# State-space stage rewritten: packed keys and queries, taps on three engines, skip as a matmul, unrolled sequence loop

## The reference, cut to what matters

```
xBC = sum((xp[:, k:k + L, :] * conv_w[:, k] for k in range(D_CONV))) + conv_b   # 4 taps
xBC = silu(xBC);  X = x * dt[..., None]
Y = (Y_diag + Y_off).reshape(b, L, NHEADS, HEADDIM) + x * D[:, None]            # skip
y = y * silu(z)
y = y * rsqrt(mean(y * y, axis=-1, keepdims=True) + EPS) * norm_w
return einsum('bld,ed->ble', y, out_proj_w)
```

## Time and profile before

| what | value |
|---|---|
| time, median of 3 runs | 1439.13 us (1433.71 to 1442.06) |
| the profiled execution's own time | 1442.29 us |
| its span, first to last instruction | 1440.5 us |
| mean granted clock of TensorE | 0.885 |
| busy PE, DVE, ACT, POOL | 83%, 59%, 50%, 23% |
| stage `L1_attn`, from the trace | 284.6 to 381.9 us |

### The profile page before, as it was taken

One profiled execution on the slowest core, in us unless ns is written; L12 is line 12 of the kernel. 1 busy time (PEld: TensorE's weight loads), 2 busy tenths in 40 slices (PEclk: granted clock), 3 DMA queues, 4 the chain that ended last, 5 costly groups with the idle time before them and its releaser, 6 DMA issues. The chain is left out here.

```text
span 1440.5 us, 24196 instructions
## 1 busy us (share of the span) xinstructions
PE 1195.0 (83%) x8927; PEld 763.0 (53%) x8928; DVE 853.4 (59%) x2086; ACT 723.1 (50%) x1459; POOL 326.6 (23%) x337
## 2 busy tenths in 40 slices
PE   6997995459698996777887973989889988897998
PEld 4664553237465664336734743856434444465776
DVE  3564564767676547787786888358452555573111
ACT  2563552341275224586677772456566542564332
POOL 1333100013211003654556440130000034300000
PEclk9999897567899998687997995799899988899999
DMA  7000000010000000000000000061094800000000
GB/s 287 1 2 2 1 2 0 24 66 1 0 2 2 1 0 1 0 1 2 2 1 1 2 1 2 1 261 67 1 198 107 170 1 1 1 2 1 1 1 15
DMA packets 15203, 44.33 MB, mean 31 GB/s; under 512 B 1872, under 2 KB 4976, under 8 KB 14448
## 3 DMA queue, kind: packets, MB, share of 16 engines
q1 hardware_dynamic: 15088, 42.80, 10.0%
HBM read 42.01 MB, written 0.79 MB: 30 GB/s over the span
## 5 line engine op out<-in xcount | busy, mean ns | idle before, releaser
L863 DVE TENSOR_REDUCE L_xattn_top<-banks 128x4 f32<-128x512 f32 x128 | 80.7, 672 | 32.6 <-PE banks L709 32.6
L815 ACT ACTIVATE L_xattn_p<-L_xattn_p 128x512 f32<-128x512 f32 x128 | 76.0, 630 | 23.8 <-DVE L_xattn_p L868 23.7
L868 DVE TENSOR_TENSOR L_xattn_p<-banks,L_xattn_top 128x512 f32<-128x512 f32 x128 | 82.4, 686 | 4.8
L823 ACT ACTIVATE L_xattn_pT<-banks 128x512 f32<-128x512 f32 x128 | 70.0, 595 | 18.3 <-PE banks L722 18.0
L722 PE MATMUL banks<-w_const,L_xattn_p 128*128 128x128 f32 x512 | 70.4, 279 | 8.1 <-ACT L_xattn_p L815 8.1
L1398 DVE TENSOR_TENSOR L_ffn_a<-L_ffn_a,L_ffn_share 128x512 f32<-128x512 f32 x64 | 39.8, 685 | 60.5 <-DMA L_ffn_share<-L_ffn_shares 37.8
L709 PE MATMUL banks<-L_xattn_ks,L_xattn_qT 32*128 32x512 f32 x256 | 71.8, 647 | 1.8 <-ACT L_xattn_ks L799 1.1
L1631 ACT ACTIVATE L_ffn_aT<-banks,L_ffn_shift 128x512 f32<-128x512 f32 x64 | 43.3, 687 | 58.9 <-PE banks L1583 57.3
L1312 PE MATMUL banks<-L_ffn_a,region_a 128*128 128x512 f32 x136 | 68.4, 608 | 4.6 <-DVE L_ffn_a L1398 4.6
L1644 DVE SCALAR_TENSOR_TENSOR x<-banks,L_ffn_combine,x 128x128 f32<-128x128 f32 x64 | 18.1, 344 | 88.6 <-PE banks L1594 88.6
L1303 PE MATMUL banks<-hT,region_a 128*128 128x512 f32 x136 | 70.1, 622 | 0.0
(11 more groups left out here) (509 smaller groups left out, 2961.0 us busy)
## 6 DMA issues: line engine op xcount, KB each, us to landing
L_ffn_share<-L_ffn_shares SPq DMA_DIRECT2D x32, 512.0 KB, 9.7
region_b<-in_L_ffn SPq DMA_DIRECT2D x1, 6216.0 KB, 29.5
region_a<-in_L_ffn SPq DMA_DIRECT2D x1, 4416.0 KB, 13.4
region_b<-in_L_attn SPq DMA_DIRECT2D x1, 3150.5 KB, 10.3
region_a<-in_L_ffn SPq DMA_DIRECT2D x1, 3080.5 KB, 21.4
region_b<-in_L_attn SPq DMA_DIRECT2D x1, 1633.5 KB, 10.0
region_b<-in_L_xattn SPq DMA_DIRECT2D x1, 835.0 KB, 10.8
w_tables<-in_tables SPq DMA_DIRECT2D x1, 832.0 KB, 13.7
```

The lines of the kernel that those rows point to most:

```text
L815: nc.scalar.activation(p[:, m % 4, :], p[:, m % 4, :], ACT.Exp, scale=scale).then_inc(exped, 1)
L823: nc.scalar.activation(pT[:, n % 2, 2 * (P % 2) + e, :], tps[e][:], ACT.Copy).then_inc(pT_kept, 1)
L863: nc.vector.tensor_reduce(top[:, i, :], rows_of(score[i][:], 4), X, ALU.max)
L868: nc.vector.tensor_tensor(rows_of(p[:, i, :], 4), rows_of(score[i][:], 4), bc(top[:, i, :], 2, T), ALU.subtract).then_inc(centered, 1)
```

## The change

Only `state_space` is changed. The key and query tiles of sequences 0 to 3 go to partitions 0 to 63 and those of 4 to 7 to 64 to 127 (`bc2`), so each is 512 columns wide; small matmuls copy the constants to both halves. ACT scales by the last tap while it leaves PSUM; DVE adds the other three taps from PSUM for both of these tiles and for one tile of `x`; for the other, ACT writes all four scaled copies and POOL adds them. The skip is a product with a diagonal matrix, accumulated in PSUM with the sum. The square with its row sum is on ACT; the mean and the power are on POOL; the norm weight is folded into `w_out`; the row scale is applied in the last addition. The sequences run unrolled in one block, with more buffers and another order, and the first half of the next stage's norm is made at the end. The removed lines are those printed above; of the added ones the core:

```diff
@@ -2246,21 +2246,51 @@
...
+    xc = st.sb("xc", [128, 2, B, T])
+    bc2 = st.sb("bc2", [128, 2, 4, T])
+    scratch = st.sb("scratch", [128, 3, B, T])
...
+    const_bank, dt_bank, bc_bank = bank[6], bank[7], bank[0:2]
+    x_banks = (banks[:, 2:4, :].rearrange("p a (b t) -> p (a b) t", t=T), banks[:, 4:6, :].rearrange("p a (b t) -> p (a b) t", t=T))
+    z_bank = (bank[6], bank[7], bank[0], bank[1])
+    mixed, seg, sums, yps, out = bank[2:4], bank[4:6], bank[0:2], bank[6], bank[7]
+    G_AT, X_AT, LAST = 0, T, T + DI
+    INIT_AT, Y_AT = 0, DI
...
+            def add_taps():
+                for i in range(3):
+                    s = TAPS - 1 - i
+                    if i == 0:
+                        pool.wait_ge(pool_tapped, 4)
+                    else:
+                        pool.drain()
+                    last = nc.gpsimd.tensor_tensor(xc[:, 1, :, s:T], xc[:, 1, :, s:T], scratch[:, i, :, 0:T - s], ALU.add)
+                last.then_inc(pooled, 1)
+
+            def stage_decays(n):
+                if n >= 2:
+                    pool.wait_ge(exponents, n - 1)
+                nc.gpsimd.tensor_tensor(later[:, n % 2, :, :], bc(g.tables["gt"], 1, NH), bc(a[:, n, :], 2, T),
+                                        ALU.mult).then_inc(later_ready, 1)
...
+            add_taps()
+            pool.wait_ge(rates_ready, 1)
+            pool.wait_ge(g.tables.loaded, 16)
+            for s in range(B + 4):
+                if s < B:
+                    stage_decays(s)
+                if s == 10:
+                    ahead.invert(pool, 0)
+                if 0 <= s - 4:
+                    invert_norm(s - 4)
...
+            def copy_consts():
+                for half in range(2):
+                    rows, at = slice(DS * half, DS * half + DS), 0
+                    for source in (w["conv_w"][0:DS, 2 * TAPS:4 * TAPS], w["conv_b"][0:DS, 2:4], w["init"]):
+                        cols = source.shape[1]
+                        nc.tensor.matmul(const_bank[rows, at:at + cols], g.ident[0:DS, 0:DS], source, start=True, stop=True)
+                        at += cols
+                for j in range(2):
+                    last = nc.tensor.transpose(dt_bank[:, 128 * j:128 * j + 128], w["norm_w"][:, 128 * j:128 * j + 128], g.ident)
+                last.then_inc(consts_made, 1)
...
+            def project_bc(half):
+                norm.await_kept(pe, half)
+                for k in range(2):
+                    at = 2 * 128 + k * DS
+                    last = nc.tensor.matmul(bc_bank[k][DS * half:DS * half + DS, :], w["w_conv"][:, at:at + DS],
+                                            g.hT[:, half * HALF:(half + 1) * HALF], start=True, stop=True)
+                last.then_inc(proj, 1)
...
+            def start_sequence(n):
+                u, rows = n % 2, half_rows(n)
+                if n == 0:
+                    pe.wait_ge(silu_ready, 4)
+                    pe.wait_ge(g.tables.loaded, 16)
+                pe.wait_ge(later_ready, n + 1)
+                if n >= 2:
+                    pe.wait_ge(pairs, n - 1)
+                    pe.wait_ge(decay_ready, n - 1)
+                nc.tensor.matmul(mixed[u][:, G_AT:G_AT + T], bc2[rows, 0, n % 4, :], bc2[rows, 1, n % 4, :], start=True, stop=True)
+                nc.tensor.matmul(mixed[u][:, LAST:LAST + NH], g.tables["le"], a[:, n, :], start=True, stop=True)
+                for h in range(NH):
+                    nc.tensor.matmul(seg[u][:, h * T:(h + 1) * T], later[:, u, h, :], g.tables["le"], start=True, stop=True)
+                for j in range(2):
+                    last = nc.tensor.transpose(mixed[u][:, X_AT + 128 * j:X_AT + 128 * j + 128], xc[:, j, n, :], g.ident)
+                last.then_inc(exponents, 1)
+
+            def sum_sequence(n):
+                u, rows = n % 2, half_rows(n)
+                if n == 0:
+                    pe.wait_ge(z_kept, 4)
+                    pe.wait_ge(skips_ready, 1)
+                if n >= 2:
+                    pe.wait_ge(y_ready, n - 1)
+                nc.tensor.matmul(sums[u][:, INIT_AT:INIT_AT + DI], bc2[rows, 1, n % 4, :], twice[rows, 2 * TAPS + 2:TWICE],
+                                 start=True, stop=True)
+                for j in range(2):
+                    nc.tensor.matmul(sums[u][:, Y_AT + 128 * j:Y_AT + 128 * j + 128], xc[:, j, n, :], skips[:, j, :],
+                                     start=True, stop=False, skip_group_check=True)
+                    if j == 0:
+                        pe.wait_ge(pairs, n + 1)
+                    for h in (2 * j, 2 * j + 1):
+                        last = nc.tensor.matmul(sums[u][:, Y_AT + h * DH:Y_AT + (h + 1) * DH], decay[:, n % 3, h, :],
+                                                xdt[:, n % 3, h * DH:(h + 1) * DH], start=False, stop=True, skip_group_check=True)
+                last.then_inc(summed, 1)
...
+            def project_out(n):
+                pe.wait_ge(yT_kept, n + 1)
+                if n == 0:
+                    pe.wait_ge(out_ready, 1)
+                else:
+                    pe.wait_ge(added, n)
+                for j in range(2):
+                    last = nc.tensor.matmul(out[:, 0:D], yT[:, n % 2, j, :], w_out[:, j, :], start=(j == 0), stop=(j == 1))
+                last.then_inc(made, 1)
...
+            copy_consts()
+            norm.turn(pe, 0, bank[4])
+            project_bc(0)
+            norm.turn(pe, 1, bank[5])
+            make_rates()
+            project_bc(1)
+            project_x(1)
+            project_x(0)
+            for m in range(4):
+                make_z(m)
+            for s in range(B + 6):
+                if 0 <= s - 5 < B:
+                    project_out(s - 5)
+                if 0 <= s - 4 < B:
+                    turn_outputs(s - 4)
+                if 0 <= s - 2 < B:
+                    sum_sequence(s - 2)
+                if s < B:
+                    start_sequence(s)
+                if s == 11:
+                    pe.wait_ge(decay_ready, B)
+                    ahead.turn(pe, 0, seg[0])
...
+            def scale_x(j):
+                act.wait_ge(proj, 4 - j)
+                if j == 1:
+                    for i in range(3):
+                        nc.scalar.activation(scratch[:, i, :, :], x_banks[1], ACT.Copy, scale=taps_of(1, i)).then_inc(pool_tapped, 1)
+                nc.scalar.activation(xc[:, j, :, :], x_banks[j], ACT.Copy,
+                                     scale=taps_of(j, 3)).then_inc(pool_tapped if j == 1 else tapped, 1)
...
+            def exp_decays(n):
+                act.wait_ge(exponents, n + 1)
+                if n >= 3:
+                    act.wait_ge(summed, n - 2)
+                if n >= 4:
+                    act.wait_ge(y_ready, n - 3)
+                nc.scalar.activation(decay[:, n % 3, :, :], rows_of(seg[n % 2][:], NH), ACT.Exp)
+                nc.scalar.activation(decay0[:, n % 4, :], mixed[n % 2][:, LAST:LAST + NH], ACT.Exp).then_inc(decay_ready, 1)
...
+            def square(n):
+                act.wait_ge(y_ready, n + 1)
+                if n >= 2:
+                    act.wait_ge(rms_ready, n - 1)
+                nc.scalar.activation(sq[:, n % 2, :], y[:, n % 2, :], ACT.Square, accum_out=meansq[:, n:n + 1]).then_inc(squared, 1)
...
+            keep_consts()
+            norm.keep(act, 0, bank[4])
+            norm.keep(act, 1, bank[5])
+            scale_bc(0)
+            scale_bc(1)
             act.wait_ge(abs_ready, 1)
             nc.scalar.activation(e[:], e[:], ACT.Exp, scale=-1.0).then_inc(e_ready, 1)
+            scale_x(1)
             act.wait_ge(u_ready, 1)
             nc.scalar.activation(log_u[:], u1[:], ACT.Ln).then_inc(log_ready, 1)
+            scale_x(0)
+            silu_bc(0)
+            silu_bc(1)
             for m in range(4):
+                keep_z(m)
+            silu_x(0)
+            silu_x(1)
+            for s in range(B + 5):
+                if s < B:
+                    exp_decays(s)
+                if 0 <= s - 4 < B:
+                    keep_yT(s - 4)
+                if 0 <= s - 3 < B:
+                    square(s - 3)
+                if s == 11:
+                    ahead.keep(act, 0, seg[0])
...
+            def add_taps(tile):
+                for i in range(3):
+                    s = TAPS - 1 - i
+                    if i > 0:
+                        dve.drain()
+                    else:
+                        dve.wait_ge(tapped, 3 if tile == 0 else tile - 1)
+                    to = xc[:, 0, :, s:T] if tile == 0 else bc2[:, tile - 2, :, s:T]
+                    source = x_banks[0] if tile == 0 else rows_of(bc_bank[tile - 2][:], 4)
+                    last = nc.vector.scalar_tensor_tensor(to, source[:, :, 0:T - s], taps_of(tile, i), to, ALU.mult, ALU.add)
+                last.then_inc(convolved, 1)
...
+            def make_pairs(n):
+                u = n % 2
+                dve.wait_ge(decay_ready, n + 1)
```

(52 more changed lines are left out.)

301 lines of the change are left out of this document (100 added, 201 removed).

## The result

The changed kernel is slower: 1457.91 us in the median of 4 runs (1454.23 to 1462.39) against 1440.06 for the kernel before in the same comparison (1433.71 to 1442.06). The ratio is 1.0133, 95% interval 1.0084 to 1.0182. The forecast was 1421.2 us with a range of 1411 to 1434, so sign and size are both wrong. The profiled execution took 1461.45 us with a span of 1459.6 and a mean granted clock of 0.870 (before: 1442.29, 1440.5, 0.885). In all that follows the ratios and their intervals leave out executions more than 1.5% above the fastest of the same kernel (three of ten where the additions come later), while medians and ranges hold all of them.

The account below looks back on a forecast made before the run. DVE was taken to end the preparation and pace the sequences at the full clock, PE at the low clock. Gains 5.2 + 11.9 + 0.8 = 17.9 us from the 1439.1 us median gave 1421.2 us, range 1411 to 1434.

Parts of the forecast that it names:

- T1: End of `project_bc(1)` in the preparation, behind which all taps hang; forecast 300.3, or 299 to 302.7 depending on the clock.
- Preparation, 5.2 us forecast: Stage work before the first sequence: ACT's chain ends last, PE starts at 316.5 instead of 321.7; bounds 2.8 and 6.5.
- the 2.1 us for the rates: Preparation step on DVE: the rates follow ACT's Ln and take 2.1 us, ending at T1+9.8.
- rival 3: POOL's sums in the preparation slowed by DVE to 4 us each, first sequence 3.5 us later, 1424.7 us; chance 0.1.
- The stop, 1.35 us: PE's wait before the output projection in steps 5 to 8, for ACT's exponentials and `keep_yT`; 1.35 us each.
- The loop, 48.4 us forecast: Sequences from the first start to the last addition: 48.4 us against 60.25, gain 11.9, full step 5.65 us.
- with the low clock for 10 us as before: Assumption for the sequence loop: its first 10 us run at the low clock, as in the old loop.
- the 76%: PE's busy share in a new full loop step, 4.3 of 5.65 us, from which the full clock was taken as kept.
- Rival 2: PE bounds the sequence loop at the low clock throughout: loop 76.8 us, 10.6 us slower in all, 1450; chance 0.06.
- Its point of decision: Change loses if the loop behind its first 10 us is at the low clock over some two thirds of the time.
- The next stage, 0.8 us: From the last addition to the next stage's first reduction: 8.83 us against 9.67, gain 0.8, bounds 0 and 1.5.

Follow-up runs that it names:

- additions come later: Changed kernel with POOL's three additions waiting until the rates are ready; median 1435.92 us, ratio 0.9972 to the kernel before.
- the repetition: The changed kernel run again without any edit, for more runs; 1455.85 us, ratio 1.0099 to the kernel before.
- two and with four copies: Changed kernel with two or four in-place ACT copies between the last two Silus, starting the loop later; medians 1438.05 and 1453.34 us.
- busy entry: Changed kernel with five unused 512-column products filling PE's wait ahead of the first sequence; 1425.39 us, ratio 0.9903 to the kernel before.
- short products: Changed kernel with sixteen unused 128-column products ahead of the first sequence, in place of five of 512; 1424.92 us, ratio 0.9894.
- products too early: Changed kernel with five unused 512-column products placed 10 us earlier, ahead of the gate projections; 1455.5 us, ratio 1.0099.
- one copy: Changed kernel with one in-place ACT copy between the last two Silus, starting the loop later; median 1448.86 us, range 1436.15 to 1461.37.
- three copies: Changed kernel with three in-place ACT copies between the last two Silus; median 1458.64 us, none of six runs below 1455.

## Why the prediction was wrong, point by point

- **End of the first projections, T1.** Forecast 300.3; ACT's first scaled copy starts at 300.08. The number is right by luck. The constants were done at 286.7 instead of 289.3, the second half of the norm at 294.7 instead of 296.0 and the step sizes at 296.8 instead of 298.6; then the last projections took 3.3 us instead of 1.7, because the clock fell again (0.56 from 296.7 to 300.1).
- **Preparation, 5.2 us forecast, 1.7 measured.** The step that failed is the 2.1 us for the rates; they took 5.9 (307.96 to 313.86). I had looked at what DVE does to POOL, and rival 3 had it the wrong way round: POOL's additions weren't slowed (2.18 us each against 2.00 taken), but two of DVE's small products took 1.80 and 2.03 us beside them. Moving the additions removed this. The rule of the Trainium skill ("SBUF — State Buffer", "Who interferes with whom") that I quoted names an exclusion for the whole length and agrees with the trace; I priced only one of its two sides. Even the 1.7 us hung on the clock: in the repetition the step sizes take 3.55 us at 0.50 instead of 1.92 at the full clock, and the preparation takes 37.4 us from the stage's first DVE instruction to the first sequence, against 35.7 in the first profile and 37.1 before. There nothing is gained.
- **The stop, 1.35 us.** Measured 1.43 before PE's weight load at the low clock, 1.26 and 1.03 (load and product) at the full one, in the place named. Right. Taking it away gains 20 us in the median though its five stops add up to 6.6 us at most, so the rest comes through the clock.
- **The loop, 48.4 us forecast, 78.1 measured.** Here the prediction failed. Two sentences of it did: "with the low clock for 10 us as before" and, after the 76% that is "nearer to the second", "So I take it as kept to the drain". I took the busy share of PE as what decides the clock and copied the old entry to a new start. But the clock never came, with PE busy 28.00 of 28.00 us. My own rows warned of it: in the earlier trace rows PE is busy 13.40 of 13.40 us at 0.50, so a full busy share had not brought the clock up there for 13.4 us. With the entry at the full clock the loop takes 46.4 us and a step 6.0 against 5.65. My 48.4 held 10 us at the low clock; without them it would be about 43.4 (an estimate, at half speed), so the durations were some 7% too short as well: PE's own work in a step is 4.72 us, not 4.3. That is 3 us; the level is worth the 31.7 us between 46.4 and 78.1.
- **Rival 2 is what happened.** It gave a step of 9.95 us and a loop of 76.8; measured are 10.16 and 78.1. It gave 1450 us in all; the preparation's missing 3.5 us, 1.3 in the loop and the scatter behind the stage make up most of the rest. I gave it 0.06 because the old loop had been low for 21.4 of 50 us only. I had not asked whether the rise near 331.8 in the earlier trace rows would come to another stream with another start.
- **Its point of decision** was the share of the low clock, some two thirds of the time behind the first 10 us. This did not hold. The loops that come up at 340 to 343 take 56.7 and 56.5 us and are low for 12 to 13 of the 46 to 47 us behind the first 10, about a quarter; by my 28 us for all of it such a kernel would be some 10 us faster (an estimate), and they are level with the one before (ratios 0.9972 and 0.9978). What was missing is the preparation's gain and the longer steps. Those entered at the full clock are 1% faster.
- **The next stage, 0.8 us.** Measured 0.75 (8.92 against 9.67). Right, with PEclk at 0.50 for all of that way in the changed kernel and until 386.3 before. In the kernels with two and with four copies, where it is 1.00 there, the same way takes 7.1 us.

Shown is: the loop's clock makes the loss (busy entry with wide and with short products, and the control with the products too early); the stop adds its own time and delays the rise; DVE held by POOL costs 2.35 us net; whether the loop comes up changes with the start (on chip 6, ten of ten against four of ten). That this last dependence recurs is supported and not shown. Its mechanism is open: no run shows what the chip counts, and why a stretch of steady work stays low at one start and not at another isn't explained. That runs without a profile came up or not is inferred from their times, and the profile that comes up after 68 us shows how rough that is.

## What to carry to other kernels

Ahead of a loop that PE bounds, read the granted clock at its first product, and don't forecast its rise from PE's busy share: one program, with one copy, took 1436 in one execution and 1461 in another, and with a start moved by a further 1.1 us the same stream stayed below 1442 in all ten. If PE stands before such a loop, idle products until the first real one are cheap to try, and order the engine that PE waits for so that the loop has no stop; together with the later additions they took 28 us off the old kernel here, of which the stage's own profile accounts for 21. When work goes to POOL, look at the small two-operand DVE instructions beside it, not only at the large ones.

## What the runs showed of the hardware that was not expected

- PE busy without a gap in the records (28.00 of 28.00 us) can stay at 1.2 GHz: in all 10 runs of the changed kernel by their times, and to the end of the loop in the profiles of it, its repetition and the kernel with three copies.
- Entered at 2.4 GHz, the same loop stayed there through stops of 1.03 us in every full step (PE busy 8.01 of 10.00 us in one window); the old loop lost it after a stand of 1.68 us with 8.09 of 9.74 busy. So PE's busy share (80% and 83%) didn't tell the two apart.
- A DVE product of 128x32, 0.13 to 0.19 us alone, took 1.80 and 2.03 us beside POOL's additions of 128x1000, while those stayed at 6.55 us for three.
- Each `ACTIVATE` that also sums rows is followed by a readout of 0.19 to 0.21 us on ACT; it lay beside PE's work and cost nothing.
